# A two-layer transformer block: layer 1's decays and half step 3 ahead of the rotary block, and attention 1's first jobs between the tiles of the down projection

## What is computed

```python
x = x + attn0(LN(x)); x = x + mamba0(ctx_1024, LN(x)); x = x + ffn0(LN(x))
x = x + attn1(LN(x)); x = x + mamba1(ctx_1024, LN(x)); x = x + moe(LN(x))
# attn0: windowed, q/k rotated (RoPE), then q, k, v normalized per head of 32 (no gain), scores
#        through tanh; attn1: causal, 16 heads of 128, q/k normalized with gains, then rotated
# mamba, per batch, channel (256) and state n (16):
#   h[t] = h[t-1] * exp(delta[t] * A[n]) + (delta[t] * u[t]) * B[n, t];  y[t] += C[n, t] * h[t]
# its u, delta, B, C come from ctx_1024 alone; then y = (y + D * u) * silu(LN(x))
# ffn0: down(silu(g * gate(x)) * (u * up(x))) * d ; moe: 32 experts of which 6 are taken, and a shared one
```

## Time and profile before

| | |
|---|---|
| three executions | 910.98, 913.36, 916.4 us |
| the profiled execution | 913.75 us, its span 912.0 us, mean granted TensorE clock 0.924 |
| TensorE busy | 767.7 us (84%), 3984 matmuls |
| VectorE busy | 703.3 us (77%) |
| ScalarE busy | 445.6 us (49%) |
| GpSimd busy | 340.6 us (37%) |
| chain that ended last | TensorE 50%, VectorE 26%, "issue" 11%, ScalarE 9% |
| stages, from the span's start | layer 0's attention with its scans to 230, gate and feed-forward to 335, attention 1 with layer 1's scans to 673, gate and experts to the end |

### The profile page before, as it was taken

How to read it: one execution, slowest core, us unless ns; L and a number is a source line. 1 busy time by engine, 2 the same in 40 slices (tenths; PEclk the granted TensorE clock), 3 DMA queues, 4 the chain that set the end, 5 groups by cost and what they waited for, 6 DMA issues and landing times.

```text
span 912.0 us, 12288 instructions
## 1 busy us (share of the span) xinstructions
PE 767.7 (84%) x3984; PEld 563.1 (62%) x3984; DVE 703.3 (77%) x1229; ACT 445.6 (49%) x928; POOL 340.6 (37%) x242
## 2 busy tenths in 40 slices
PE   6771459877798996799999999999955799999997
PEld 2241346554433563477767776777743689999996
DVE  4869779889857976999999999999977544444443
ACT  1663368650336402666566556756642354444442
POOL 1001346552330422233333323432343286666663
PEclk9785579998799998999999999999987899999999
DMA  4313223345020212011111211111300243334431
GB/s 171 121 47 114 93 94 125 115 139 218 1 98 0 74 43 92 19 40 44 51 36 36 69 36 36 55 39 36 118 0 1 79 158 138 138 138 138 141 135 46
DMA packets 28884, 74.63 MB, mean 82 GB/s; under 512 B 3633, under 2 KB 6337, under 8 KB 28449
## 3 DMA queue, kind: packets, MB, share of 16 engines
q1 hardware_dynamic: 28384, 71.51, 23.2%
q10 hardware_dynamic: 448, 2.49, 0.8%
HBM read 72.55 MB, written 1.44 MB: 81 GB/s over the span
## 4 chain that ended last, share of the span: by engine, by line
PE 50%; DVE 26%; issue 11%; ACT 9%; POOL 3%; DMA 1%; POOLq 0%; DVEq 0%; SPq 0%; ACTq 0%
PE ps L1671 6%; PE ps L1785 6%; PE ps L1786 6%; PE ps L1787 6%; PE ps L1631 4%; DVE hS L976 3%; PE ps L1651 3%; PE ps L1750 3%; PE ps L1435 2%; PE ps L1738 2%; DVE arena L1280 2%; DVE hS L1006 2%; DVE ps L968 2%; PE ps L1408 1%; PE ps L1720 1%
## 5 line engine op out<-in xcount | busy, mean ns | idle before, releaser
L403 POOL TENSOR_TENSOR hS<-hS,BCb 128x512 f32<-128x512 f32 x64 | 81.6, 1278 | 131.9 <-issue 66.7
L1387 DVE SCALAR_TENSOR_TENSOR arena<-ps,arena 128x1024 f32<-128x1024 f32 x32 | 39.2, 1224 | 102.2 <-ACT arena L842 93.1
L426 POOL TENSOR_TENSOR hS<-hS,BCb 128x1024 f32<-128x1024 f32 x23 | 56.1, 2440 | 111.3 <-DVE ps L968 96.3
L1671 PE MATMUL ps<-WB,hT 128*128 128x512 f32 x192 | 88.0, 603 | 3.0 <-DVE arena L1261 2.0
L476 POOL TENSOR_TENSOR MHl<-arena,MHh 128x1024 fp32r<-128x1024 f32 x34 | 81.7, 2404 | 16.9 <-ACT MHh L845 16.9
L1416 PE MATMUL ps<-ident,hS 128*128 128x128 f32 x256 | 40.1, 311 | 54.7 <-POOL hS L426 31.2
L1785 PE MATMUL ps<-Wh,MHh 128*128 128x256 f32 x272 | 77.8, 286 | 6.0 <-POOL MHl L476 6.0
L1006 DVE TENSOR_TENSOR_SCAN hS<-dA,ps 128x512 f32<-128x512 f32 x64 | 78.1, 1220 | 2.2
L1786 PE MATMUL ps<-Wl,MHh 128*128 128x256 f32 x272 | 77.6, 285 | 0.0
L1787 PE MATMUL ps<-Wh,MHl 128*128 128x256 f32 x272 | 77.5, 285 | 0.0
L1416 PEld LDWEIGHTS ps<-ident,hS 128*128 128x128 f32 x256 | 32.6, 159 | 65.1 <-POOL hS L426 38.2
(11 more groups left out here) (233 smaller groups left out, 1967.4 us busy)
## 6 DMA issues: line engine op xcount, KB each, us to landing
BCb<-bc_dram SPq DMA_DIRECT2D x32, 512.0 KB, 3.7
BCb<-bcq_dram SPq DMA_DIRECT2D x64, 256.0 KB, 3.1
arena<-gate_dram SPq DMA_DIRECT2D x32, 512.0 KB, 3.7
WB<-in_we SPq DMA_DIRECT2D x34, 256.0 KB, 2.7
WB<-in_wqkv SPq DMA_DIRECT2D x1, 3072.0 KB, 12.7
WA<-in_wo ACTq DMA_DIRECT2D x1, 2048.0 KB, 7.7
WA<-in_ffn SPq DMA_DIRECT2D x1, 1408.0 KB, 7.9
pkb<-in_pk SPq DMA_DIRECT2D x2, 698.0 KB, 4.7
```

Source lines behind the costliest of these rows:

```text
L403: gp.tensor_tensor(h, h, qbc(q)[:, 1:2, :].broadcast_to([P, DT, S]), ALU.mult).then_inc(s["c_ready"], 1)
L426: gp.tensor_tensor(h, h, BCb[g % SB_LOADS][:, 1:2, :].broadcast_to([P, DT, HALF]), ALU.mult).then_inc(s["c_ready"], 1)
L1671: last = mm(ps[:, bank + t, :], hT[:, c, P * (2 * b + t):P * (2 * b + t) + P], WB[:, c, c0:c0 + 512], start=(c == 0), stop=(c == HC - 1))
```

## The change

1. ScalarE of layer 0: decays 1 to 3 directly behind the first; the second pair's copy, softplus and Ln behind them.
2. VectorE of layer 0: half step 3 ahead of the rotary block; three Newton rounds instead of four.
3. `tables()` goes into the gate/up loop. Half 1's residual, statistics, normalization and transposes go into attention 1's list; four more quarter steps run ahead of it (`Q_IN_FFN` 14).
4. TensorE: down tiles 0 to 5, half 0's transposes, tile 6, the projections of jobs 0 and 1, tile 7, the eight products left, V. Jobs 0 and 1 get buffers of their own (parts of the packed weights, `H`, `ctxp`), and half 1's transposes use banks 0 and 1.
5. A written-out start (`ramp`) takes the place of the jobs at negative units; the jobs behind it start two units later or one.
6. The mask is added to the two diagonal blocks of a unit's scores alone, not to the block of zeros between them.

```diff
 QRING = 8
-Q_IN_FFN = 10
-Q_GROUP_ENDS = (1, 3, 7, 9, QSTEPS - 1)
+Q_IN_FFN = 14
+Q_GROUP_ENDS = (1, 7, 8, 9, 13, QSTEPS - 1)
...
-        job_bank = lambda j: 2 if j == 1 else 0
-        job_a = lambda j: JA[j % 2]
-        job_b = lambda j: V1[1] if j == 1 else JB
-        job_s = lambda j: (QT[1].rearrange("p h q -> p (h q)").rearrange("p (t n) -> p t n", t=2)) if j == 1 else SQ
-        v_bank = lambda b: 0 if b else 4
+        tok2 = lambda a: a.rearrange("p (t n) -> p t n", t=2)
+        JA_FIRST = [tok2(ar(24, 1024)), tok2(pkb[:, 0:1024])]
+        JB_FIRST = [tok2(ar(28, 1024)), tok2(H[:, 0:4, :].rearrange("p a b -> p (a b)"))]
+        JS_FIRST = [tok2(ar(36, 1024)), tok2(ctxp.rearrange("p b s -> p (b s)")[:, 0:1024])]
+
+        job_bank = lambda j: 4 if j == 1 else 0
+        job_a = lambda j: JA_FIRST[j] if j < 2 else JA[j % 2]
+        job_b = lambda j: JB_FIRST[j] if j < 2 else JB
+        job_s = lambda j: JS_FIRST[j] if j < 2 else SQ
+        v_bank = lambda b: 0 if b else 2
...
         TR_LNS = [0, 2, 3, 5]
-        TR_BANK = [(4, 6), (0, 2), (0, 4), (0, 2)]
+        TR_BANK = [(4, 6), (0, 2), (0, 0), (0, 2)]
         CONV_BANK = [0, 4]
...
                 times_cq(q)
-            ln_rstd(3, (1,))
...
                     job(JOB[a])
+                elif kind == "stats1":
+                    ln_rstd(3, (1,))
                 elif kind == "dbu" and a > Q_IN_FFN:
...
             d_u(0)
+            steps_to(3)
             xdbl_copy(1)
-            steps_to(1)
             softplus(1)
             softplus_ln(1)
-            steps_to(2)
             for t in range(NT):
...
                 sc.copy(Q0[:, t, :], ps[:, 4 + t % 4, 0:NQKV0]).then_inc(s["qkv0_copied"], 1)
-            steps_to(3)
             d_u(1)
...
             delta_u(1)
+            ssm_step(3)
             dve.wait_ge(s["qkv0_copied"], NT)
...
             v.tensor_tensor(QKV0, QKV0, heads0(st0[:, 0, :]), ALU.subtract).then_inc(s["rope0_rot"], 1)
-            for g in range(3, 6):
+            for g in range(4, 6):
                 ssm_step(g)
...
             ch.link(v.tensor_scalar(st0[:, 2, :].bitcast(I32), st0[:, 2, :].bitcast(I32), -1.0, float(0x5F3759DF), ALU.mult, ALU.add))
-            for k in range(4):
+            for k in range(3):
                 ch.link(v.tensor_tensor(st0[:, 3, :], st0[:, 2, :], st0[:, 2, :], ALU.mult))
...
                 last = v.scalar_tensor_tensor(st0[:, 2, :], st0[:, 3, :], 1.5, st0[:, 2, :], ALU.add, ALU.mult)
-                if k < 3:
+                if k < 2:
                     ch.link(last)
...
                     w1_means()
+                if j == 3:
+                    tables()
                 if j == PREP_DT + 1:
...
             ln_stats(3, 0)
-            quarters(step, 2)
+            quarters(step, 1)
             ln_apply(3, 0)
-            tables()
-            fd_residual(1)
-            ln_stats(3, 1)
+            quarters(step, 1)
             ln_tr_copy(2, 0)
-            ln_apply(3, 1)
+            quarters(step, 4)
...
                     job(*a)
+                elif kind == "fd1":
+                    fd_residual(1)
+                elif kind == "stats1":
+                    ln_stats(3, 1)
+                elif kind == "apply1":
+                    ln_apply(3, 1)
                 elif kind == "ln1":
...
-            def fd(hf):
-                for t in range(4 * hf, 4 * hf + 4):
+            def fd(*tiles):
+                for t in tiles:
                     for i in range(NI):
                         m = mlen(i)
-                        last = mm(ps[:, FD_BANK[hf] + (t % 4) // 2, 256 * (t % 2):256 * (t % 2) + 256], hid0[0:m, i, P * t:P * t + P], WDN[0:m, i, :],
+                        last = mm(ps[:, FD_BANK[t // 4] + (t % 4) // 2, 256 * (t % 2):256 * (t % 2) + 256], hid0[0:m, i, P * t:P * t + P], WDN[0:m, i, :],
                                   start=(i == 0), stop=(i == NI - 1))
...
-            fd(0)
+            fd(0, 1, 2, 3)
             for k in range(4):
                 accq(next(step))
-            fd(1)
-            for q in step:
-                accq(q)
+            fd(4, 5)
             ln_tr(2, (0,))
+            fd(6)
             ln_ready(2, 0)
...
                     pe.wait_ge(s["job_tr_copied"], 2 * JOB[b[:2]] + 2)
+                elif was == "ln1":
+                    ln_ready(2, 1)
                 else:
...
                 if b == 0:
-                    ln_ready(2, 1)
+                    pe.wait_ge(s["x_new"], XN_FFN)
                 banks_free("v", b)
...
                 j = JOB[b, i]
-                if j == 1:
-                    pe.wait_ge(s["x_new"], XN_FFN)
                 banks_free("proj", (b, i))
...
                 pe.wait_ge(s["job_tr_copied"], 2 * max(JOB[b, 0], JOB[b, 1 + g]) + 2)
+                if u == 0:
+                    pe.wait_ge(s["v_copied"], 1)
                 if u >= 2:
...
                 q, k = QT[(4 * b + g) % 2], KT[b % 2]
-                mm(ps[:, 2 + p, 0:3 * P], identb[:], mask1[:], start=True, stop=True, skip_group_check=True)
+                diagonal = lambda z: z.rearrange("p (k n) -> p k n", k=3)[:, 0::2, :]
+                mm(diagonal(ps[:, 2 + p, 0:3 * P]), identb[:], diagonal(mask1[:]), start=True, stop=True, skip_group_check=True)
                 mm(ps[:, 2 + p, 0:P], q[:, h % REP1, 0:P], k[:, g, 0:P], start=False, stop=True, skip_group_check=True)
...
                     pe.wait_ge(s["at1_copied"], u)
-                else:
-                    pe.wait_ge(s["v_copied"], 1)
                 for x in range(3):
...
                     v_job(a)
+                elif kind == "fd7":
+                    fd(7)
+                    for q in step:
+                        accq(q)
                 elif kind == "ln1":
+                    banks_free("ln1", 0)
                     ln_tr(2, (1,))
...
-    rope_job(-8, 0, 0, 2, 3)
-    rope_job(-7, 0, 1, 2, 3)
-    at(-7, "wo1", 0)
-    at(-6, "ln1", 0)
-    v_job(-5, 0)
+    first, second = (0, 0), (0, 1)
+    both = lambda j: [(kind, j + (x,)) for x in range(2) for kind in ("tr", "trc")]
+    ramp = [("proj", first), ("sq", first), ("proj", second), ("sq", second), ("fd7", 0),
+            ("rot", first), ("sum", first), ("rot", second), ("fd1", 0), ("sum", second),
+            ("v", 0), ("vc", 0), ("wo1", 0), ("rope", first)] + both(first) + [("rope", second)] + both(second)
+    rope_job(-1, 0, 2, 2, 3)
+    rope_job(2, 0, 3, 2, 4)
+    rope_job(4, 0, 4)
+    at(4, "stats1", 0)
+    at(6, "apply1", 0)
+    at(11, "ln1", 0)
     for b in range(B):
         u = H1 * b
-        rope_job(u - 3, b, 2)
-        rope_job(u, b, 3)
-        rope_job(u + 3, b, 4)
+        if b:
+            rope_job(u - 3, b, 2)
+            rope_job(u, b, 3)
+            rope_job(u + 3, b, 4)
         if b + 1 < B:
...
     total = sum(price(p) for u in range(units) for p in parts.get(u, [])) + sum(price(p) for p in ssm)
-    plan = []
+    plan = ramp
     behind = []
...
             plan += [("pt", u - 1), ("ptc", u - 1)]
-        plan += pick("wo1", "rope", "rot", "sum")
+        plan += pick("rope", "rot", "sum", "stats1", "apply1")
         for kind, m in now:
...
-    claims = [p for p in ATT1_PLAN if p[0] in ("proj", "v") or (p[0] == "tr" and p[1][2] == 0)]
-    claims = [p for p in claims if p != ("v", 0) and (p[0] == "v" or p[1][:2] != (0, 1))]
+    claims = [p for p in ATT1_PLAN if p[0] in ("proj", "v", "ln1") or (p[0] == "tr" and p[1][2] == 0)]
+    claims = [p for p in claims if p != ("v", 0) and (p[0] in ("v", "ln1") or p[1][:2] != (0, 1))]
     before = {}
```

## The result

| | before | after |
|---|---|---|
| median of 20 executions | 913.59 us | 918.04 us |
| span of the profiled execution | 912.0 us | 916.1 us |
| TensorE, VectorE busy | 767.7, 703.3 us | 766.9, 707.4 us |
| granted TensorE clock, mean | 0.924 | 0.921 |
| chain that ended last | TensorE 50%, VectorE 26% | TensorE 39%, VectorE 38% |

The changed kernel is slower: its time is 1.0041 times that of before, 95% interval [1.0028, 1.0055]. I had said 912.3, with 904 to 918 as the range: wrong sign, and 0.04 us outside.

A forecast was written before the change was run, and what follows sets the result against it. It took VectorE to bound attention 1, busy 39.1 of 40 us. Layer 0's -4.1 us and attention 1's +3.0 summed to -1.1: 912.65 us for the profiled execution, 912.3 for the median, range 904 to 918.

The forecast's parts named there:

- Part A: Layer 0, items 1 and 2: earlier decays and half step 3, one Newton round fewer; -4.1 us, between -5.4 and -2.9.
- Behind it the order is as before: Layer 0 from scan 4 on: order unchanged, so the 3.2 us won there stay, plus 0.9 for the Newton round.
- Rival 3: Layer 0: half step 3 only moves, the decay wait takes back 3.2, only Newton's 0.9 us left; total +2.1, chance 0.10.
- Part B: Start and list of attention 1, items 3 to 6: +3.0 us, with bounds of -4.6 and +10.0.
- Start of the rotation: VectorE at attention 1's start: the first rotation starts at 335.7 instead of 339.63, -3.9 us.
- Work behind: VectorE behind the first rotation: four quarter steps fewer, but half 1's residual, statistics and normalization more; -3.4 us.
- Waits of the start: VectorE up to the fourth rope: 11.1 us of waits against 8.4 before, +2.7 us.
- Units 8 to 11: Attention 1 behind the fourth rope: waits for a norm, rotation (1,1) and the copy of hT, 1.05 + 2.2 + 2.3 = +5.5 us.
- Units 15 and 47: Attention 1, units with only 1.2 us of VectorE work: the norm waits for the exp, +2.1 us together.
- Rival 1: Attention 1: the lead is kept, waits of units 8 to 47 don't come; total -8.7, 904.7 us, chance 0.30.
- Rival 2: Attention 1: TensorE's clock falls in pauses, two projections take 7.0 instead of 3.5 us; total +5.9, 919.3, chance 0.10.
- At nothing: Attention 1 edits priced at no cost or gain: shorter masks, moved tables, the later WO load, broadcast loads.

The follow-up runs named there:

- b_only: Items 3 to 6 of the change alone, on the kernel before, with its old layer 0: ratio 1.0078 to the kernel before, 7.1 us slower.
- tables_only: The kernel before with only the ten table products moved into the gate/up loop: ratio 1.0004 to the kernel before.
- early_third: The changed kernel with the third job's projection, square, rotation and sum moved ahead, the projection directly behind the first job's transposes: ratio 0.9971 to the kernel before.
- even_units: The changed kernel with quarter steps dealt so no unit has only norm and maximum, at most two per batch 0 unit, three later: 1.0017 of the kernel before.
- spread_even: `even_units` with the rope of job (0,4) one unit earlier, so no unit has both a rope and the next rotation: ratio 0.9985 to the kernel before.
- best: The changed kernel plus `early_third`, `spread_even`, one quarter step ahead of the third rotation, and layer 0's decays 4 to 7 before QKV's square: 0.9920 of before.
- best2: `best` with ScalarE's six decays behind the first job's transposed copies, and VectorE's copy of half 1's transposed stream behind the quarter step: 0.9883, 902.26 us.
- mask_only: The kernel before with only the mask edit, adding it to the two diagonal blocks alone: ratio 1.0000 to the kernel before.
- a_only: Items 1 and 2 of the change alone, on the kernel before, with its old attention 1: ratio 0.9976 to the kernel before, 2.2 us faster.

## Why the prediction was wrong

Many of the mechanisms were found, but the terms were too small and erred the same way, and two steps failed outright: that a lead won in layer 0's head passes attention 0 whole, and that only VectorE's work per unit counts in the new list. I go through them by the text.

**Part A, forecast -4.1, measured -2.2 alone.** The times of layer 0's head held: scan 2 at 45.6 (46.34), rotary block at 59.7 (59.44), scan 4 at 80.75 (80.62) with a wait of 4.40, the last Newton operation near 93.2 (93.00). Of the three places for the table load the one that I took, directly ahead of the decay, was right. One of these times came out by luck. I had the rotary block wait for the copies of QKV, up to 59.7, with TensorE's second half at the 7.09 us of before. In the changed kernel it took 5.40,

```profile
50.47 5.40 PE L1507 MATMUL ps<-WB,hT 128*128 128x384 f32 x16 [0.32 <-ACT arena L659]
```

and the last copy ended at 56.4. What set the block's start was VectorE's own half step 3, without any wait.

The step that failed is "Behind it the order is as before", by which all 4.1 us would have arrived. The order is as before, but by the means of the traces a lead of 4.7 us becomes 3.0 in attention 0 (2.8 in the changed kernel's), and in the time 2.2 are left. The losses stand mostly where TensorE's pieces run at half rate; whether the earlier work brings that about is open. I had not looked there at all, though TensorE's clock in that stretch stands in the page. Rival 3 was wrong: scan 4 starts 3.36 us earlier (83.98 against 80.62), so more than Newton's round is left.

**Part B, forecast +3.0, measured +7.1 alone, and by the ledger of the changed trace +8.4.** Term by term, in that trace:
- Start of the rotation -3.9: it starts 6.4 earlier, of which A's 2.8 are no part: -3.6. Right (`b_only` has -4.9). That the tables' 3.7 us were won there was wrong (`tables_only`).
- Work behind -3.4: from the first rotation to the residual the old trace has 333.97 us, 15.4 of them waits; the new one 346.01 with 30.3. Work went from 318.5 to 315.7: -2.9. Right in sum, but I credited it ahead of rope 4, where the new list has 2.1 us more work (half 1's residual and one more unit's norm and maximum); the 5.0 less stand behind. That is why rope 4 ends no earlier: -6.4 at the start, +4.5 of waits, +2.1 of work.
- Waits of the start 11.1: 12.9 are there, 1.16, 3.60, 4.56 and 3.60 for my 1.1, 2.6, 3.9 and 2.8. Each is larger, three of them by 0.7 to 1.0; the 0.7 for GpSimd is absent. +4.5 instead of +2.7. Slow pieces stand in front of all three: the first scores took 1.7 us (0.95 at full rate in `early_third`), the third projection 4.33 and not 3.5, the third job's transposes 1.97 instead of 1.09.
- Units 8 to 11, +5.5: 0.98 + 2.13 + 2.18 = 5.3. Right in size, and in cause half right: I named the bunch in units 6 and 7 and the unit of 1.2 us behind it. `even_units` took the short unit away and left 1.32 and 2.18; `spread_even` parted the rope from the rotation, and of these 1.33 is left.
- Units 15 and 47, +2.1: 0.98 + 1.27 = 2.25. Right.
- Not forecast, and the largest miss: 2.51 + 2.07 = 4.6 near 521 and 530, the result copy that moved into a full unit of ScalarE. I had counted VectorE's work per unit and put ScalarE's queue at nothing without a reason, though a moved step counts on every queue.

So B is -3.6 - 2.9 + 4.5 + 10.4 (17.4 - 7.0 behind rope 4) = +8.4, which is the 5.65 at the residual and A's 2.8. At the residual my -1.1 should thus have been +5.6. The span is 4.1 longer and the ratio says 3.7 us: behind the residual this execution was 1.5 us quicker than that of before, and such executions scatter by as much there.

**The rivals.** Rival 1, the lead kept, does not hold: none of those waits stayed away. Rival 2, the clock, had 0.10 of the chances: it gave 919.3, and 918.04 came. By the ratio (+3.7 us) the time lies between its +5.9 and rival 3's +2.1, so the number does not decide for it. Its mechanism is there in part, smaller at each place than I had it (the third projection at 4.33 instead of 7.0 us) and at more places; the projection near unit 8 ran at full rate, 3.60. Here are two pauses with slow pieces behind them in the changed kernel's TensorE (VectorE did not wait for the projection of 4.56):

```profile
362.33 0.90 PE L1740 MATMUL ps<-ident,arena 128*128 128x128 f32 x3 [2.41 <-DVE arena L1302]
...
369.26 4.56 PE L1681 MATMUL ps<-WB,hT 128*128 128x512 f32 x8
...
401.44 0.66 PE L1446 MATMUL ps<-ident,ACC 128*128 128x128 f32 x4 [2.45 <-ACT ACC L617]
```

My argument against this rival, that the same work of before ran at full rate but for short pieces, misread the trace. Behind a pause of 4.69 us V's projection took 5.33 us there:

```profile
347.54 1.97 PE L1708 MATMUL ps<-ident,arena 128*128 128x128 f32 x8 [4.69 <-DVE arena L1280]
349.30 5.33 PE L1671 MATMUL ps<-WB,hT 128*128 128x512 f32 x8
```

The `best` and `best2` pair shows that a longer pause and a slower projection come together and what they cost. How much of B's +7.1 is clock and how much is plain waiting was not separated at the start: `early_third` takes away pauses and slow pieces in one. Near 415 `even_units` says more: at a clock of 1.00, 3.5 of the changed kernel's 4.3 us of waits for rotation (1,1) and the copy of hT are still there, so most of them are plain waiting there.

**At nothing.** Masks and tables: right. The wait for WO and the broadcast loads don't show.

## What to carry to other kernels

In a part where two engines hand small pieces to each other, count the waits of a new order at the slower clock too: a pause of TensorE can be paid once as a wait and again in the pieces behind it. And don't carry a lead through such a part whole: here 4.7 us became 3.0, and 9.5 became 7.7. When a list is shifted, read the queue of every engine unit by unit, above all the one that is "half idle"; here six decays in front of two small copies on ScalarE cost 3.5 us, and one result copy in a full unit goes with 4.6 us of VectorE's waits. A hole is worth filling only when the instruction behind it does not wait for something else: of 5.3 us of filled holes, 1.0 arrived in the time, while moving the one projection that the hole waited for brought 6.4.

## What the runs showed of the hardware

TensorE went to half rate behind pauses of 2.38 to 2.57 us (transposes 0.90 instead of 0.49, a projection 5.40 instead of 3.70), while behind one of 2.00 in `best2` it was at full rate (the mask's matmul 0.28), and behind one of 1.85 in `even_units`, too. The length of the last pause alone does not tell. Behind the same pause of 2.41 us three transposes took 0.90 in the changed kernel (362.33) and 0.55 in `even_units` (362.75), where only the pieces behind them were slow. In the changed kernel the eight transposes behind a pause of 2.27 us still took 1.10, full rate, and the scores behind them, 0.73 us later, ran at half rate (two of their matmuls 1.06 instead of 0.60).

When the clock comes back also differs between kernels with the same layer 0. The four kernels with the old layer 0 reach full rate in attention 0 at 134.5 (`before`, `tables_only`), near 137 (`mask_only`) and near 139 (`b_only`); with part A it is 132.3 in the changed kernel and `early_third` and 135.1 in `a_only`. Within each group scan 11 of VectorE started at the same time to within 1.4 us. I had not expected that. What sets it was not tried, and it is one reason why one trace is good to 2 us only.
